# Exact pieces of x by truncation, cut in the stages that make x, and attribute one-hots as weights

## The reference, cut to what matters

```python
def _L0_gnn_ref(...):                       # four layers
    agg = segment_sum(x[src], dst, N)
    h = (1.0 + eps[i]) * x + agg
    h = relu(_bn(h @ W1[i] + b1[i], ...)); h = _bn(h @ W2[i] + b2[i], ...)   # batch norm over nodes
    ...
    x = h + x_in                            # then a layer norm and two dense layers
def _L1_gnn_ref(...):                       # one layer; row, col = src, dst
    messages = x[col] @ W_T_w.T + W_T_b + temporal_features @ T_w.T + T_b
    return relu(x @ W_S_w.T + W_S_b + segment_sum(messages, row, N))
def _L2_gnn_ref(...):                       # four layers
    msg = relu(x[src] + ea)
    h = x + segment_sum(msg, dst, N)
    h = silu(h @ W1[l] + b1[l]) @ W2[l] + b2[l]
    x = layer_norm(x + h) * gamma[l] + beta[l]
def _L3_gnn_ref(...): ...                   # attention over the edges, once
```

## Time and profile before

| | |
|---|---|
| median of 3 runs | 10419.15 us (10417.22 to 10422.83) |
| profiled execution | 10417.13 us |
| its span | 10415.4 us |
| mean granted TensorE clock | 0.817 of full |

### The profile page before, as it was taken

How to read it: one execution, slowest core, us unless ns; L and a number is a source line. 1 busy time by engine, 2 the same in 40 slices (tenths; PEclk the granted TensorE clock), 3 DMA queues, 4 the chain that set the end, 5 groups by cost and what they waited for, 6 DMA issues and landing times.

```text
span 10415.4 us, 240438 instructions
## 1 busy us (share of the span) xinstructions
PE 7541.2 (72%) x64204; PEld 6497.3 (62%) x64205; DVE 7092.3 (68%) x16971; ACT 3677.0 (35%) x7598; POOL 4975.9 (48%) x4705
## 2 busy tenths in 40 slices
PE   4799990388786886883689778777776885666664
PEld 3467660277675775773589776666765765555553
DVE  5577770366766766666556589789798797666664
ACT  0122220230612504304520454644645644444443
POOL 0777776336064072370035137056074173777772
PEclk7555555699898998996899899899898998666665
DMA  8766665997584874960699489598696894666666
GB/s 339 199 211 210 212 211 31 111 293 219 212 288 119 324 242 153 330 188 13 174 325 384 188 330 366 208 345 308 252 356 232 322 366 161 161 164 160 164 160 79
DMA packets 1747196, 2371.77 MB, mean 228 GB/s; under 512 B 516388, under 2 KB 1046151, under 8 KB 1746651
## 3 DMA queue, kind: packets, MB, share of 16 engines
q1 hardware_dynamic: 1292446, 1275.33, 39.0%
q0 software_dynamic: 318912, 1049.17, 31.2%
q10 hardware_dynamic: 135677, 45.42, 1.9%
HBM read 1485.10 MB, written 955.49 MB: 234 GB/s over the span
## 4 chain that ended last, share of the span: by engine, by line
PE 19%; DVE 9%; POOL 7%; issue 7%; ACT 4%; DMA 3%; SPq 2%; DVEq 2%; ACTq 0%; POOLq 0%
PE ps L848 8%; PE ps L827 7%; POOL big L739 7%; DVE gath L1526 3%; ACT gath L1110 3%; DMA big<-kv_table,src_at 2%; PE ps L851 2%; SPq L613 2%; ACT big L1245 1%; DVE onehot L1481 1%; DVE heads L1599 1%; DVE gath L1595 1%; ACT gath L1082 0%; DVE gath L1610 0%; PE ps L977 0%
## 5 line engine op out<-in xcount | busy, mean ns | idle before, releaser
L729 POOL DMA_INDIRECT gath<-msg_units,unit_at_d x2176 | 2329.4, 1071 | 3263.2 <-DMA msg_units<-gath 2579.2
L848 PE MATMUL ps<-onehot,gath 128*128 128x125 f32 x18224 | 2585.0, 287 | 620.6 <-ACT gath L1110 347.4
L848 PEld LDWEIGHTS ps<-onehot,gath 128*128 128x128 f32 x18224 | 2219.4, 193 | 977.3 <-issue 528.0
L827 PE MATMUL ps<-big,onehot 125*128 x29376 | 1795.4, 221 | 862.3 <-DVE onehot L1481 694.8
L827 PEld LDWEIGHTS ps<-big,onehot 125*128 125x128 bf16 x29376 | 1695.3, 98 | 965.3 <-issue 934.0
L1082 ACT ACTIVATE gath<-ps 128x512 f32<-128x512 f32 x2448 | 1393.2, 596 | 726.0 <-PE ps L827 571.5
L1519 DVE TENSOR_TENSOR onehot<-iota,node_d 128x500 f32<-128x500 f32 x2176 | 1464.4, 673 | 169.2 <-PE ps L848 109.9
L1481 DVE TENSOR_SCALAR onehot<-row_b,part 125x512 bf16<-125x512 uint8 x2448 | 1129.5, 482 | 606.4 <-PE ps L827 582.9
L739 POOL DMA_INDIRECT big<-kv_table,src_at x1088 | 1094.1, 1006 | 532.2 <-issue 295.6
L701 POOL DMA_INDIRECT rec<-big,idx_ring x832 | 974.5, 1171 | 279.9 <-issue 241.2
L1533 DVE TENSOR_TENSOR big<-big,ps 128x125 f32 x2448 | 685.4, 280 | 546.7 <-PE ps L848 375.8
(11 more groups left out here) (223 smaller groups left out, 9121.9 us busy)
## 6 DMA issues: line engine op xcount, KB each, us to landing
msg_units<-gath SPq DMA_DIRECT2D x2176, 256.0 KB, 2.3
big<-ea_units SPq DMA_DIRECT2D x1088, 256.0 KB
ea_units<-rec SPq DMA_DIRECT2D x16, 4352.0 KB, 53.2
rec<-gath SPq DMA_DIRECT2D x272, 256.0 KB, 6.2
big<-rec SPq DMA_DIRECT2D x272, 256.0 KB
big<-in_attr_t SPq DMA_DIRECT2D x208, 256.0 KB
rec<-big SPq DMA_DIRECT2D x1, 43296.0 KB, 152.4
gath<-msg_units,unit_at_d POOLq DMA_INDIRECT x2176, 5.3
```

Source lines behind the costliest of these rows:

```text
L729: pool.indirect_dma_start(att_slot(q) if way == "attr" else gath[:, q, :], None, units, bass.IndirectOffsetOnAxis(ap=unit_at[w][:, g:g + 1 ...
L827: ins = pe.matmul(ps[:, r, c], hots_t[0:NT, r, c], big16[0:NT, ds(at_[q] + (2 * HT + k) * NODES_PAD, D)], start=k == 0, stop=k == 2)
L848: ins = pe.matmul(ps[:, RING + r, 0:NT], x, hots[:, r, j, :], start=j == 0, stop=j == UNIT - 1)
```

## The change

The pieces are cut by truncation. The upper 16 bits of an f32 word are a bf16 number, so the first piece is x itself, read at every second bf16 element; one subtraction leaves the rest in f32 words, whose upper halves are the second piece; a second subtraction leaves the last piece, also in f32 words. TensorE reads upper halves of words in NA, REST and LOW; REST and LOW lie in HT and AC, shifted by 150 columns. ScalarE has no part in it.

The two subtractions, for one fifth of x at a time (1280 columns), are done on VectorE in the stage that makes x: in `norm_out` of sum layers 0 to 2, and in the `layer_norm` ahead of the attr pass, ahead of the msg passes, and of msg layers 0 to 2. The first pass still cuts at its head. In `norm_out` the loop of VectorE is written out, for all five uses.

In the attr pass the one-hots are weights, and 194 columns of a record (128 and 66) are the moving operand: four matmuls a group in place of eight. The sums come out by node, and two `to_t` stages turn them.

```diff
+    do("to_t", AC, D, 0, RE)
+    do("to_t", HT, D, 0, AC)
-    do("linear", [(("ws", 0), XT), (("wt", 0), AC), ("attr", HT)], ACT.Relu, "s_b", AC, None, None)
+    do("linear", [(("ws", 0), XT), (("wt", 0), RE), ("attr", AC)], ACT.Relu, "s_b", AC, None, None)
...
+        upper = big[:, :].bitcast(BF16).rearrange("p (n t) -> p n t", t=2)[:, :, 1]
+        REST, LOW = HT * NODES_PAD - EARLY, AC * NODES_PAD - EARLY
...
+        def without_upper(dve, src, dst, k):
+            src, dst = (slice(b + k * FIFTH_W, b + (k + 1) * FIFTH_W) for b in (src, dst))
+            return dve.tensor_tensor(big[0:NT, dst], big[0:NT, src], upper[0:NT, src], ALU.subtract)
+        def cut(dve, src, k):
+            without_upper(dve, src * NODES_PAD, REST, k).then_inc(rest_made, 1)
+            cuts[0] += 1
+            dve.wait_ge(rest_made, cuts[0])
+            without_upper(dve, REST, LOW, k).then_inc(low_cut, 1)
...                                                     # TensorE, picks
-                            for k in range(3):
-                                ins = pe.matmul(ps[:, r, c], hots_t[0:NT, r, c],
-                                                big16[0:NT, ds(at_[q] + (2 * HT + k) * NODES_PAD, D)],
-                                                start=k == 0, stop=k == 2)
+                            for b in (NA * NODES_PAD, REST, LOW):
+                                ins = pe.matmul(ps[:, r, c], hots_t[0:NT, r, c], upper[0:NT, ds(at_[q] + b, D)],
+                                                start=b == NA * NODES_PAD, stop=b == LOW)
+                pe.wait_ge(low_cut, FIFTHS * (n["edges"] + 1))
...                                                     # TensorE, sums
+                            if way == "attr":
+                                x = att_slot(q)[:, j * REC + AT_EA:j * REC + AT_EA + D + AX]
+                                ins = pe.matmul(ps[0:NT, RING + r, 0:D + AX], hots[:, r, j, :], x,
+                                                start=j == 0, stop=j == UNIT - 1)
...                                                     # ScalarE, head of a pass
-                for k in range(PARTS + 1):
-                    if k < PARTS:
-                        act.activation(piece(0, k), x_part(k), ACT.Copy).then_inc(high_cut, 1)
-                    if k:
-                        act.wait_ge(rest_made, cut_before + k)
-                        act.activation(piece(1, k - 1), x_rest[0:NT, (k - 1) % 2, :], ACT.Copy).then_inc(middle_cut, 1)
...                                                     # VectorE, head of a pass
+                if n["edges"] == 0:
+                    for b in (REST, LOW):
+                        dve.memset(big[0:NT, b + NTILES * D:b + BKT * D], 0.0)
+                    for k in range(FIFTHS):
+                        cut(dve, NA, k)
...                                                     # VectorE, sums of the attr pass
+                    if way == "attr":
+                        a, z = (big[0:NT, ds(at_ + b * NODES_PAD, w_)] for b, w_ in ((AC, D), (HT, AX)))
+                        dve.tensor_tensor(a, a, ps[0:NT, RING + r, 0:D], ALU.add)
+                        ins = dve.tensor_tensor(z, z, ps[0:NT, RING + r, D:D + AX], ALU.add)
...                                                     # VectorE, norm_out
+                def pieces(i):
+                    dve.wait_ge(mm_free, base + SLOTS_PS * (i + 1))
+                    cut(dve, NA, i)
+                for i in range(SWEEPS):
+                    for j in range(i * SLOTS_PS, (i + 1) * SLOTS_PS):
+                        dve.wait_ge(act_blk, n["applied"] * NBLK + j + 1)
+                        x = T(XT)[:, j * BLK:(j + 1) * BLK]
+                        dve.tensor_tensor(x, x, T(dst)[:, j * BLK:(j + 1) * BLK], ALU.add).then_inc(added, 1)
+                    if then_cut and i:
+                        pieces(i - 1)
+                if then_cut:
+                    pieces(SWEEPS - 1)
...                                                     # VectorE, layer_norm, for each fifth
+                    if then_cut:
+                        dve.wait_ge(ln_fifth, 5 * n["scaled"] + i + 1)
+                        cut(dve, b, i)
```

More of the change, by code:

```diff
@@ L64 @@
 MAGIC = 12582912.0
-PARTS = 4
-assert NODES_PAD % (2 * PARTS) == 0
+FIFTHS = 5
+FIFTH_W = NTILES // FIFTHS * D
+EARLY = NTILES * (D - NT)
+assert N <= NODES_PAD - EARLY
 BLK = 2 * NT
@@ L128, in network @@
         do("norm_apply", HT, AC, act, (f"obn_g{l}", f"obn_b{l}"))
-        do("norm_out", AC, HT, act, None)
+        do("norm_out", AC, HT, act, l < LAYERS - 1)
     do("layer_norm", NA, D, ("ln_g", 0), ("ln_b", 0), False, AC, None, False)
@@ L159, in network @@
     do("attend")
-    do("norm_out", RE, HT, ACT.Identity, None)
+    do("norm_out", RE, HT, ACT.Identity, False)
     do("layer_norm", NA, D, None, None, False, None, "out", False)
@@ L451, in program @@
         block = ctx.enter_context(nc.Block())
[L453 to L457, removed]
+        def without_upper(dve, src, dst, k):
+            src, dst = (slice(b + k * FIFTH_W, b + (k + 1) * FIFTH_W) for b in (src, dst))
+            return dve.tensor_tensor(big[0:NT, dst], big[0:NT, src], upper[0:NT, src], ALU.subtract)
+        cuts = [0]
+        def cut(dve, src, k):
[3 more added lines that the diff above has]
+            without_upper(dve, REST, LOW, k).then_inc(low_cut, 1)
         def walk(eng, **mine):
@@ L475, in do @@
                     names.append("io")
-                if kind == "norm_out" and args[3] or kind == "layer_norm" and args[6]:
+                if kind == "layer_norm" and args[6]:
                     names.append("io_fifths")
@@ L506, in program @@
         SUM_D, SUM_S, NAT_D, NAT_S, ATT_D = range(5)
-        own = {"sum": ("s", NAT_S, "d", SUM_D), "msg": ("s", NAT_S, "d", SUM_D), "attr": ("d", NAT_D, "s", SUM_S)}
+        own = {"sum": ("s", NAT_S, "d", SUM_D), "msg": ("s", NAT_S, "d", SUM_D), "attr": ("d", NAT_D, "s", NAT_S)}
         PASSES = ("sum",) * LAYERS + ("attr",) + ("msg",) * LAYERS
@@ L846, in sums @@
                         for j in range(UNIT):
-                            x = att_slot(q)[:, j * REC + AT_EA:j * REC + AT_EA + D] if way == "attr" else unit_ring[:, q, j, :]
-                            ins = pe.matmul(ps[:, RING + r, 0:NT], x, hots[:, r, j, :], start=j == 0, stop=j == UNIT - 1)
-                        if way == "attr":
-                            for j in range(UNIT):
-                                ins = pe.matmul(ps[0:AX, RING + r, P:P + NT],
-                                                att_slot(q)[:, j * REC + AT_A64:j * REC + AT_A64 + AX], hots[:, r, j, :],
+                            if way == "attr":
+                                x = att_slot(q)[:, j * REC + AT_EA:j * REC + AT_EA + D + AX]
+                                ins = pe.matmul(ps[0:NT, RING + r, 0:D + AX], hots[:, r, j, :], x,
+                                                start=j == 0, stop=j == UNIT - 1)
+                            else:
+                                ins = pe.matmul(ps[:, RING + r, 0:NT], unit_ring[:, q, j, :], hots[:, r, j, :],
                                                 start=j == 0, stop=j == UNIT - 1)
@@ L1200, in end_of, with norm_out @@
                 act.nop(nofuse=True).then_inc(stage_done, 1)
-            def norm_out(n, src, dst, func, tab):
+            def norm_out(n, src, dst, func, then_cut):
                 base = n["blocks"] * NBLK
```

55 lines of the change are left out of this document (15 added, 40 removed).

## The result

The changed kernel takes 10397.3 us (median of 20 runs, 10381.3 to 10421.2) against 10417.4 us for the kernel before on the same chip (20 runs, 10404.9 to 10432.4): a ratio of 0.9979, 95% interval 0.9973 to 0.9986. It is faster by 20 us where 131 were forecast; the forecast of 10288 us and its range (10262 to 10350) both missed. One execution of one experiment (e_contig) took 17469 us where its three others took 10244 to 10255, and the numbers given for it leave it out.

What follows compares the result with a forecast made beforehand. It took TensorE, busiest at 72%, and the nine edge passes to bound the kernel. Part 1's 106 us, Part 2's nothing and Part 3's 25 made 131 off 10417.1, plus 2 for the median: 10288 us, range 10262 to 10350.

Steps and rivals of the forecast that it cites:

- Part 1: Ahead of the passes: cutting x moves into the stages that make x, on VectorE; a gain of 106 us.
- norm_outs: Sum layers 1 to 3: VectorE alternates cuts and adds, first matmul 10.4 us earlier each; 31 us.
- two plain layer norms: Layer norms without scaling, ahead of attribute and msg passes: cuts fit while VectorE idles; 16.2 us each, 32 together.
- msg norms: Three msg layer norms: cuts join VectorE's multiplies and adds, 6.08 us a fifth; 12.4 us each, 37 together.
- first pass: Head of the first pass: cuts on VectorE alone needn't wait for ScalarE's row loads; 3.5 us gained.
- Part 3: Attribute sums: fewer matmuls until gathers bind, 40 us gained, less 15 us for two to_t stages; nets 25 us.
- Rival B: Attribute sums: gathers hold at 387 GB/s, so the one-hot change only costs; 10328 us, chance 0.09.
- Part 2: Pick matmuls: reading strided upper halves of 4-byte words costs nothing, 59 ns a matmul as before.
- Rival A: Pick matmuls: a strided column costs TensorE time, 26 us for each ns, up to 11,700 us; chance 0.13.
- All else: Start, other sums, turns and tail taken together; a gain of 6 us forecast.

Runs made afterwards that it cites:

- e_contig: Changed kernel with all three pick matmuls reading the third piece, written as adjacent bf16 values, at one address a group; 10248.5 us, ratio 0.9847.
- e_attr_half: Changed kernel with two of the four attribute-sum matmuls of each group left out, gathers the same; 10383.8 us.
- e_b5: Kernel before, adjacent pieces kept, with pick addresses taking five register operations and not three; 10527.7 us, ratio 1.0122.
- e_addr3: Changed kernel with tile offsets stored doubled, so pick addresses take three register operations and not five, same strided reads; 10337.2 us, ratio 0.9933.
- e_align: Changed kernel with the second and third piece starting at a multiple of 16 bytes (EARLY 148 for 150); 10383.0 us, one execution.
- e_strides: Changed kernel with columns of the three pieces read 8, 16 and 4 bytes apart; 12373.5 us.
- e_two4: e_addr3 with pick laps of 16 groups and tile offsets loaded four at a time, every four groups; 10250.8 us, ratio 0.9844.
- e_b_two4: Kernel before with only 16-group pick laps and offsets loaded four at a time; run on another chip, ratio 0.9949.

## Why the prediction was wrong

- **Part 1, the cut moves: right.** For the norm_outs, the two plain layer norms and the msg norms 31 + 32 + 37 us were forecast, 30, 31 and 40 came. A fifth's work in the msg norm took 5.98 us for 6.08. In the first pass the cuts took the 14.67 us of ten in a row, and 16.3 us lay between the first row load and the first matmul where 20.4 had (3.5 forecast); the work ahead of it came 3.4 us later in this execution, which hides the gain in the span.
- **Part 3, the attribute pass: right.** 477.6 to 437.7 us (-39.9 for -40) at 421 GB/s, +15.2 us for two to_t stages. e_attr_half shows the bound: the gathers, as the sum took them. Rival B falls.
- **Part 2, "I take no cost": wrong, and for a reason that it didn't consider.** It priced what TensorE reads and not what its sequencer works out before it may read. A lap was called 5.67 us of matmuls and 1.0 us of "register loads at the head", and only the first was examined. The edit turned three register operations an address into five, 24 times a lap; e_b5 shows that this alone costs 14.2 us a pass, and the eight passes together came out 94 us longer. Two things hinted at it before any run: the diff, with a slice of a view with a stride and an offset at a dynamic place, and the trace of the kernel before, where the sequencer's fused instructions and its 1.16 us load stand under the picks' and the loads' lines.
- **Rival A** named the right line and the wrong mechanism. The stride is there, 4.2 ns a matmul of 128 columns; on its own it would have cost 26,112 x 4.2 ns = 110 us if nothing else had set the lap. It costs 35 us in e_addr3 against before, and 1 us a pass where sequencer work fills the lap anyway. The sign that the prediction gave for A, 96 matmuls in 5.9 us or more, came true (6.08) and would have misled: e_align's took 5.89 and its picks stayed where they were.
- **Two slips in the working**, both small: 3.99 + 1.4 is 5.4 and not 5.3, and 10288 less 29 is 10259, where the range starts at 10262.
- **"All else"** lost 12 us where a gain of 6 was forecast, chiefly by the one pass of sums named above. That is chance of this execution, as far as is known.

The Trainium skill, "SBUF — State Buffer", section "Door 1: The DMA port swizzle", gives full rate to a reader with two or more hits in a 16-byte line. For TensorE's moving operand the trace differs in the small: 4 hits a line cost 60.0 ns for 55.8 (57.7 where the pieces start at a multiple of 16 bytes). With one hit a line, in e_strides, a matmul takes 227 ns where the other two take some 100 each at the same clock, so in the large the rule holds here.

Is the forecast gain there once the sequencer's work is equal? e_two4 stands at 0.9844 and e_b_two4 at 0.9949 of the kernel before: 1.05%, 109 us by 10417, against 131 forecast. The comparison runs over two chips, so I give it as a size and not as a measured ratio.

What stays open: why a load of the same eight offsets takes 1.16 to 1.18 us in before and e_b5 and 1.04 to 1.07 in e_addr3 and after, why a load of two offsets isn't shorter than one of four, and what holds the sequencer at 14 matmuls ahead. The last is read off three traces and was not tested by an edit.

## What to carry to other kernels

- Two chips differed by 8% on the kernel before (10417 and 11251 us). The sums took 409 to 412 us a sum pass in e_b_two4 on the slower one and 354 to 358 before, while the attribute pass's picks took 282.8 and 282.7.
